# Routed pairs of a decoder layer: the turns of the next pair's rows stand between the two down products of the older pair, not behind them

## The reference, cut to what matters

```python
E, K, D, F = 16, 2, 256, 176
def _swiglu(x, wg, wu, wd):
    return silu(x @ wg.T) * (x @ wu.T) @ wd.T

logits = flat @ gate_w.T                       # flat: 1024 x 256
probs = softmax(logits)
_, top_idx = top_k(logits + expert_bias, K)
top_w = take_along_axis(probs, top_idx); top_w = top_w / sum(top_w)
combine = sum(one_hot(top_idx, E) * top_w[..., None], axis=1)
for e in range(E):
    out = out + combine[:, e:e+1] * _swiglu(flat, w_gate[e], w_up[e], w_down[e])
out = out + _swiglu(flat, sw_gate, sw_up, sw_down)
```

## Time and profile before

| what | value |
|---|---|
| median of 3 runs | 661.34 us (659.74 to 663.22) |
| the profiled execution's own time | 660.12 us |
| its span | 658.4 us |
| granted TensorE clock, mean | 0.988 of full speed |
| busy: PE, DVE, ACT, POOL | 626.1, 531.7, 453.6, 476.4 us |

### The profile page before, as it was taken

How to read it: one execution, slowest core, us unless ns; L and a number is a source line. 1 busy time by engine, 2 the same in 40 slices (tenths; PEclk the granted TensorE clock), 3 DMA queues, 4 the chain that set the end, 5 groups by cost and what they waited for, 6 DMA issues and landing times.

```text
span 658.4 us, 12041 instructions
## 1 busy us (share of the span) xinstructions
PE 626.1 (95%) x3545; PEld 492.5 (75%) x3545; DVE 531.7 (81%) x852; ACT 453.6 (69%) x742; POOL 476.4 (72%) x456
## 2 busy tenths in 40 slices
PE   8989999999999999999999999999999989899980
PEld 6677888878888788888887888878888877555540
DVE  5999999999999999999999999976973547622346
ACT  3768788797887978879788788786422455433364
POOL 3386989879898798887987889677752573855554
PEclk9999999999999999999999999999999999999995
DMA  4162113111131111311212112043034287359554
GB/s 163 54 262 79 65 50 112 53 59 64 48 112 64 48 64 48 112 64 48 79 41 104 64 48 105 6 129 102 17 100 123 68 243 287 94 159 272 168 129 143
DMA packets 25993, 66.66 MB, mean 101 GB/s; under 512 B 4099, under 2 KB 16899, under 8 KB 23179
## 3 DMA queue, kind: packets, MB, share of 16 engines
q1 hardware_dynamic: 23131, 58.54, 26.5%
q0 software_dynamic: 2832, 7.75, 4.7%
HBM read 58.00 MB, written 9.85 MB: 103 GB/s over the span
## 4 chain that ended last, share of the span: by engine, by line
PE 82%; DVE 6%; POOL 4%; issue 3%; ACT 2%; DMA 2%; POOLq 0%; ACTq 0%; DVEq 0%
PE ps L878 38%; PE ps L892 9%; PE ps L908 7%; PE ps L893 4%; PE ps L1172 4%; PE ps L810 3%; PE ps L828 3%; DVE conv L1744 2%; PE ps L1221 2%; PE ps L852 2%; POOL conv L752 1%; PE ps L917 1%; PE ps L918 1%; POOL conv L668 1%; PE ps L1146 1%
## 5 line engine op out<-in xcount | busy, mean ns | idle before, releaser
L1744 DVE SCALAR_TENSOR_TENSOR conv<-ps,w_raw,conv 128x506 f32<-128x506 f32 (+3 forms) x352 | 320.6, 934 | 15.3 <-ACT conv L1386 9.2
L878 PE MATMUL ps<-x_hi,w_hi 128*128 128x512 f32 x384 | 158.8, 414 | 2.1 <-DVE conv L1744 1.1
L1386 ACT ACTIVATE conv<-ps,w_raw 128x512 f32<-128x512 f32 x160 | 108.2, 687 | 64.4 <-PE ps L878 63.9
L878 PE MATMUL ps<-x_hi,w_lo 128*128 128x512 f32 x384 | 151.7, 395 | 0.0
L878 PE MATMUL ps<-x_lo,w_hi 128*128 128x512 f32 x384 | 150.7, 392 | 0.0
L525 POOL TENSOR_TENSOR decay<-cum_b,cum_tok 128x512 f32<-128x512 f32 (+1 forms) x128 | 103.3, 828 | 9.4 <-DMA cum_b<-cum_scratch 9.4
L878 PEld LDWEIGHTS ps<-x_hi,w_hi 128*128 128x128 f32 x384 | 72.6, 189 | 20.2 <-issue 2.4
L531 POOL TENSOR_TENSOR decay<-decay,mask 128x512 f32<-128x512 f32 x64 | 82.7, 1292 | 5.0
L878 PEld LDWEIGHTS ps<-x_hi,w_lo 128*128 128x128 f32 x384 | 72.5, 189 | 16.8
L878 PEld LDWEIGHTS ps<-x_lo,w_hi 128*128 128x128 f32 x384 | 72.9, 190 | 12.7
L1371 ACT ACTIVATE conv<-conv 128x1024 f32<-128x1024 f32 x80 | 79.3, 1059 | 1.5 <-DVE conv L1744 1.5
(11 more groups left out here) (285 smaller groups left out, 1090.0 us busy)
## 6 DMA issues: line engine op xcount, KB each, us to landing
cum_b<-cum_scratch SPq DMA_DIRECT2D x16, 1024.0 KB, 4.7
w_raw<-in_winT SPq DMA_DIRECT2D x15, 778.0 KB, 4.3
y_all<-in_wgu SPq DMA_DIRECT2D x4, 1408.0 KB, 11.9
late<-in_wdn SPq DMA_DIRECT2D x2, 1408.0 KB
x_scratch<-conv SPq DMA_DIRECT2D x19, 128.0 KB, 4.9
late<-in_woutT SPq DMA_DIRECT2D x1, 2048.0 KB, 9.2
ys_scratch<-y_blk SPq DMA_DIRECT2D x32, 64.0 KB
res_scratch<-conv SPq DMA_DIRECT2D x11, 130.0 KB
```

Of the source, the lines that this page charges most:

```text
L878: mm = pe.matmul(ps[:, tile_bank(n, tile) + hf, :], wp[:, par, w], xp[:, kk, t], start=(i == 0), stop=(i == 5))
L1386: act.activation(conv[:, par, tile, hf * 512:(hf + 1) * 512], ps[:, tile_bank(n, tile) + hf, :], ACT.Copy, scale=w_raw[:, par, tap:tap + 1 ...
L1744: dve.scalar_tensor_tensor(out=o[:, :, s:], in0=u[:, :, 0:T - s], scalar=w_raw[:, par, c:c + 1], in1=o[:, :, s:], op0=ALU.mult, op1=ALU.ad ...
```

## The change

Two calls move up in TensorE's stream. In the ten loop turns above, `turn_block(i + 2)` and `turn_block(i + 3)` stood behind `down(i - 1)`. Now they stand between `down(i - 2)` and `read_expert`, which `down(i - 1)` follows. No instruction is added or removed. The streams of ScalarE, VectorE, GpSimd and SyncE are the same as before, and no wait of the moved instructions changes.

```diff
@@ -1304,6 +1304,9 @@
                 gate_up(i + 1)
                 if i > TBS:
                     down(i - 2)
+                    if i + 2 < ITEMS:
+                        turn_block(i + 2)
+                        turn_block(i + 3)
                 if i + 2 < ITEMS:
                     read_expert(i + 2 - TBS)
                 if i > TBS:
@@ -1314,9 +1317,6 @@
                     turn_block(TBS + 3)
                     turn_hidden(TBS + 1)
                 else:
-                    if i + 2 < ITEMS:
-                        turn_block(i + 2)
-                        turn_block(i + 3)
                     turn_hidden(i)
                     turn_hidden(i + 1)
                 if i + 2 < ITEMS:
```

## The result

| | before | changed |
|---|---|---|
| median of 4 runs | 661.27 us | 671.8 us (667.96 to 672.78) |
| ratio | 1 | 1.0146, 95% interval 1.0103 to 1.0188 |
| profiled span | 658.4 us | 669.1 us |
| the ten loop turns in the profile | 54.7 us | 65.9 us |

The change makes the kernel 1.5% slower: +10.5 us, where 7.6 were forecast. The time lies in the range. The direction and the mechanism were right, and the size was a quarter too small.

A forecast was written before the change was run, and what follows sets the result against it. TensorE was taken to bound the kernel. Each loop turn would become the landing + 2.76 us, ten 63.3 in place of 54.7: +8.6, less 1, so 661.3 + 7.6 = 668.9 us, range 663.5 to 673.0.

The forecast's parts named there:

- TensorE bounds the stage, and a loop turn of 5.35 us has nothing to give: Routed experts: TensorE is busy 9.77 and 9.99 of 10 us; all idle time in ten loop turns is 1.2 us.
- The landing's cover shrinks and closes a loop through GpSimd: Second gather of a pair: cover shrinks 0.9 us per turn; its late landing delays the hidden turns and the next gather.
- The register load loses its cover: `read_expert` behind the moved turns: reached only after the landing, 0.85 us from load to the first product behind it.
- The changes of kind: TensorE switching between whole-array transposes and half-array products: four per loop turn, not two, +0.2 to +0.3 us.
- ScalarE's copy is no longer waited for: Gate product at the head of a loop turn: its wait for the turned rows' copy goes, at most 1.1 us.
- The sum, 63.3 us less 1: Ten loop turns: 63.3 us in place of 54.7, +8.6, less 1 us, leaving +7.6 us.
- The first formula: One loop turn is 0.27 + landing + 0.85 + 1.64, the landing + 2.76 us; mean 6.3, ten 63.3 us.
- The 1 us that I took off: Deduction from +8.6 us: with longer loop turns fewer gathers fall where SyncE's expert copies fill the DMA engines.
- the mean of six landings: Gather start to landing in six loop turns shown, 2.8 to 4.4 us, mean 3.6, taken for all ten.
- The rival for which the Trainium skill is named: Loop turns: landings come in time, only changes of kind cost, +0.9 to +2.2 us, 662 to 663.5; chance 0.13.
- The signs: Changed profile: loop turns 60 to 64 us, TensorE's busy time hardly changed; wrong if landings come under 2.8 us.

The follow-up runs named there:

- fifth run: The changed kernel with every gather of GpSimd issued one loop turn earlier: 661.07 us, ratio 0.9992.
- third run: The changed kernel with the second gather of a pair no longer held until the hidden turns of the pair before are done: 664.92 us, ratio 1.0046.
- seventh run: The changed kernel unchanged, timed again on the same chip as the first six runs: 671.25 us, ratio 1.0133.
- first run: The changed kernel with the register load placed before the two moved turns, not behind them: 665.43 us, ratio 1.0065.
- second run: Against the changed kernel, only the turn of block i+2 stays moved up; that of i+3 goes behind the second down product: 663.12 us, ratio 1.0020.
- the ninth: The kernel before, unedited, profiled once more on another chip (10): 661.99 us, loop turns 56.7 us.

## Why the prediction was right

- **TensorE bounds the stage, and a loop turn of 5.35 us has nothing to give.** Right: the changed kernel with all landings covered is no faster than before.
- **The landing's cover shrinks and closes a loop through GpSimd.** Right, and the main cause: covering the landing takes the whole loss away (fifth run), and starting one gather earlier takes two thirds (third run). Of the count of 11.2 us it is the largest term, 4.9.
- **The register load loses its cover.** Right in kind and size. The prediction put it at 0.85 us from the load to the product; the rows of the fifth loop turn show 0.89 (610.0 to 610.89). Against the 0.33 us in which the product could have followed, that is some 0.5 more; the trace shows 0.49, in eight of ten loop turns (and in none with the load ahead of the turns).
- **The changes of kind, +0.2 to +0.3 per loop turn.** Right at the lower end: 0.20.
- **ScalarE's copy is no longer waited for.** Right for every gate product whose rows are turned at the new place. The one wait left, 0.6 us, stands in front of the first of the ten loop turns, and the rows for that product are turned at the old place.
- **The sum, 63.3 us less 1.** This is the mis-sized term. The first formula gave 63.3 us for ten loop turns, and the two profiles of the changed kernel show 65.9 (64.3 without the fall of the clock) and 64.0. The 1 us that I took off, because longer loop turns would leave fewer gathers in the stretch of heavy DMA traffic, did not come. The mean landing in the new order is again 3.6 us behind the gather's start, with one of 5.0 in the third loop turn. Taking the mean of six landings for all ten was right in the mean, and in part luck: single ones go from 2.7 to 5.0 us. The fall of the clock was in no term.
- **The rival for which the Trainium skill is named** (page "DMA: Bandwidth & Descriptors", section "Anatomy of one DMA"; the estimate by it is 2.3 us for a gather) did not come true. No landing in the profile of the changed kernel is under 2.7 us.
- **The signs.** The landings were not to come under 2.8 us. Two did, at 2.7 to 2.8, in the first and the eighth loop turn, and just these two took 5.55 us and did not wait; the other eight came at 3.2 to 5.0. TensorE's busy time in the stage was to hardly change, and that was wrong: it is 53.8 of the 55 us from 578 us on before, 59.3 of 66 after, and 57.5 of 64.2 in the seventh run. The fifth run, nearly without waits, shows 55.6 of 56, so about 2 of it come from the new order itself, and 1.6 in the first profile from the fall of the clock. The rest is not taken apart; the ends of the products are modelled.

The forecast was +7.6 us, the result is +10.5. Of the 2.9 between them, 1 is the deduction. The rest fits the clock: the fall cost 1.6 us in the execution that was profiled, and the two executions with a mean clock of 0.989 lie 6.7 and 7.7 us above their medians of before, at the forecast. The clock is not shown to be all of it, for the loop turns scatter by 2 us from one execution to the next.

## What to carry to other kernels

Before you move an instruction up in an in-order stream, look up when its operands land, not only whether they land in time today; and look up what paces the transfer. Here the transfer's start hung on work that stands behind the moved instruction, so the work that a late landing held up held up the next gather in its turn, and no cover was won back. The register load behind the wait cost 0.49 us in eight of ten loop turns, and nothing ahead of the wait (first run).

## What the runs showed of the hardware that was not expected

In the third loop turn of the changed kernel TensorE waited for the landing (1.53 us idle) and for the load (0.42), and then the granted clock fell to 0.50, that is 1.2 GHz. Windows of 2 us, with the columns of the earlier trace rows:

```profile
594.00:596.00 2.00, 0.44 (x2) 0.20 (x2) 0.00 (x0) 0.41 (x2) 0.58 (x1) 1.00 0.86 238
596.00:598.00 2.00, 1.89 (x11) 0.98 (x12) 0.00 (x0) 0.49 (x2) 0.00 (x0) 0.67 0.90 247
598.00:600.00 2.00, 2.00 (x9) 0.91 (x9) 0.84 (x2) 0.00 (x0) 0.95 (x1) 0.50 0.82 285
600.00:602.00 2.00, 2.00 (x16) 0.93 (x14) 0.34 (x1) 0.41 (x2) 0.95 (x1) 0.97 0.65 118
```

At half clock the four hidden turns took 1.08 us in place of 0.64, and the clock was back at 600.1. It cost 1.6 us, half in this loop turn, which took 8.6, and half in the next (6.9). In the seventh run the same place had as long a wait (1.69 and 0.42 us idle), and the clock stayed at 1.00:

```profile
596.00:598.00 2.00, 2.00 (x16) 1.14 (x18) 0.57 (x2) 0.38 (x1) 0.12 (x1) 1.00 0.91 267
```

The clock also fell ahead of the routed experts, where the edits change nothing: in the second run from 546.0 to 556.2 us, and in the ninth, the kernel before, from 542.8 to 546.2. TensorE had been busy for 5.2 of the 6.0 us and 5.8 of the 6.8 us before. So the length of the wait does not settle alone whether the clock falls. What else does stays open here.
